# Hybrid Mamba / product-key FFN / linear-attention kernel: the preparation of the FFN stages moved into the stages beside them

## The reference, cut to what matters

```
x = x + mamba(_layernorm(x))          # 512 channels, 16 states, a scan over 1024 steps
x = x + ffn(_layernorm(x))
x = x + linear_attention(_layernorm(x))
x = x + ffn(_layernorm(x))            # the same weights as the first
```

```
queries = (hidden_states @ W_q).reshape(2, n, 64)     # n = 4096 tokens; W_q is 256 x 128
routing = einsum('tnd,tdk->tnk', queries, keys)
scores2, idx2 = top_k(routing, 8)                     # and the best 8 of the 64 pair sums
ew  = silu(einsum('nh,nkh->nk', x, down_embed[indices])) * softmax(scores)
out = einsum('nk,nkh->nh', ew, up_embed[indices])
    + silu(x @ gate_w) * (x @ up_w) @ down_w
```

## Time and profile before

| what | us |
|---|---|
| median of 3 runs | 2038.39 (2036.72 to 2038.93) |
| the profiled execution, its own time | 2038.59 |
| span of its instructions | 2036.9 |
| Mamba ends (last sum into `res`) | 954.54 |
| first matmul of the first FFN loop | 1005.38 |
| last instruction of attention | 1615.51 |
| first matmul of the second FFN loop | 1644.05 |
| PE / DVE / ACT / POOL busy | 1812.9 / 1478.3 / 1054.1 / 1035.7 |

### The profile page before, as it was taken

How to read it: one execution, slowest core, us unless ns; L and a number is a source line. 1 busy time by engine, 2 the same in 40 slices (tenths; PEclk the granted TensorE clock), 3 DMA queues, 4 the chain that set the end, 5 groups by cost and what they waited for, 6 DMA issues and landing times. The chain is left out here.

```text
span 2036.9 us, 27560 instructions
## 1 busy us (share of the span) xinstructions
PE 1812.9 (89%) x9655; PEld 1418.8 (70%) x9655; DVE 1478.3 (73%) x2279; ACT 1054.1 (52%) x1773; POOL 1035.7 (51%) x612
## 2 busy tenths in 40 slices
PE   6888889888989898666799999997999699999999
PEld 2555565656565565455488888886777578888888
DVE  4899999999999999996766666663343555555555
ACT  6775767677776767342444444432333253333333
POOL 2888898989898988874311111111444511111111
PEclk9899999999999999777899999998999899999999
DMA  6222232333323232322000000000000000000000
GB/s 188 76 81 99 85 95 92 90 92 93 93 88 94 91 96 85 93 85 90 0 1 0 0 0 0 0 0 27 1 0 0 0 1 11 10 10 10 10 10 21
DMA packets 55619, 97.78 MB, mean 48 GB/s; under 512 B 10736, under 2 KB 10864, under 8 KB 54896
## 3 DMA queue, kind: packets, MB, share of 16 engines
q1 hardware_dynamic: 55536, 96.74, 15.1%
HBM read 92.00 MB, written 4.72 MB: 47 GB/s over the span
## 5 line engine op out<-in xcount | busy, mean ns | idle before, releaser
L329 POOL TENSOR_TENSOR m_U<-m_U,m_C 128x1024 f32<-128x1024 f32 x256 | 603.5, 2366 | 69.3 <-DVE m_U L751 58.9
L628 ACT ACTIVATE m_dA<-m_delta,m_negA 128x512 f32<-128x512 f32 x512 | 344.4, 685 | 177.0 <-DVE m_U L751 175.1
L456 PEld LDWEIGHTS m_y<-m_ident,m_U 128*128 128x128 f32 x2048 | 258.7, 151 | 114.5 <-issue 72.9
L751 DVE TENSOR_TENSOR_SCAN m_U<-m_dA,m_carry,m_U 128x512 f32<-128x512 f32 x256 | 312.2, 1267 | 7.0 <-ACT m_dA L628 6.6
L456 PE MATMUL m_y<-m_ident,m_U 128*128 128x128 f32 x2048 | 291.9, 290 | 25.5 <-POOL m_U L329 25.4
L751 DVE TENSOR_TENSOR_SCAN m_U<-m_dA,m_U 128x512 f32<-128x512 f32 x256 | 296.9, 1207 | 16.6 <-ACT m_dA L628 13.1
L734 DVE TENSOR_TENSOR m_U<-m_dx,m_psB 128x1024 f32<-128x1024 f32 x208 | 249.3, 1199 | 27.8 <-PE m_psB L440 27.7
L440 PE MATMUL m_psB<-m_stack,m_pick 128*128 128x512 f32 x208 | 110.8, 533 | 66.8 <-DVE m_U L734 66.4
L1100 POOL TENSOR_TENSOR gl_S<-gl_Rt 128x1024 f32<-128x1024 f32 x16 | 31.6, 1997 | 271.5 <-ACT gl_Rt L1208 271.5
L1100 POOL TENSOR_TENSOR fl_S<-fl_Rt 128x1024 f32<-128x1024 f32 x16 | 31.6, 1997 | 264.9 <-ACT fl_Rt L1208 264.9
L1428 POOL TENSOR_TENSOR a_rinv<-a_ssq,a_mhalf 128x64 f32<-128x64 f32 x8 | 84.3, 10550 | 113.5 <-DVE a_ssq L1643 113.5
(11 more groups left out here) (319 smaller groups left out, 4438.0 us busy)
## 6 DMA issues: line engine op xcount, KB each, us to landing
m_C<-bc_rows SPq DMA_DIRECT2D x256, 256.0 KB, 3.1
m_B<-bc_rows SPq DMA_DIRECT2D x48, 256.0 KB, 3.5
fq_whole<-in_ffn_w SPq DMA_DIRECT2D x4, 1024.0 KB, 8.1
out<-res SPq DMA_DIRECT2D x8, 512.0 KB, 2.8
res<-in_x SPq DMA_DIRECT2D x1, 3072.0 KB, 12.6
res<-in_x SPq DMA_DIRECT2D x2, 512.0 KB, 4.6
a_whole<-in_Wkvqu SPq DMA_DIRECT2D x1, 1024.0 KB, 4.8
m_inw<-in_in_w SPq DMA_DIRECT2D x1, 512.0 KB, 4.6
```

What stands on the lines that cost most here:

```text
L329: pool.tensor_tensor(u, u, C[:, M % C_RING, :].unsqueeze(1).to_broadcast([P, PE_E, CHUNK]), ALU.mult).then_inc(hc_ready, 1)
L456: last = nc.tensor.matmul(y[:, t, j * P:(j + 1) * P], U[:, M % U_RING, j, t * P:(t + 1) * P], ident[:, :], start=False, stop=n == N - 1, i ...
L628: nc.scalar.activation(dA[:, s % A_RING, :], delta[:, q, e, :], ACT.Exp, scale=negA[:, e, n:n + 1]).then_inc(dA_ready, 1)
L751: nc.vector.tensor_tensor_scan(u, dA[:, s % A_RING, :], u, carry[:, e, n:n + 1] if q else 0.0, ALU.mult, ALU.add).then_inc(scan_done, 1)
```

## The change

`ffn_queries` is gone. What it did is spread over three places.

1. **In Mamba's chunk 7.** SP fetches `W_q`, `keys` and the four pieces behind C of unit 231 and ahead of C of unit 232. It first waits until the buffers of chunk 6, over which the pieces are written, are free; the last of these waits is for `back3` of chunk 6, which PE does in unit 229. The mean and variance of chunks 4, 1, 5 and 0 are made on ACT (`sum`, `square`), the inverse on POOL (`asked_factors`), and their queries by `norm`, `turn0`, `turn1` and `query` on ACT and PE, at fixed units. `high0` and `high1` round two of the pieces on ACT. The other two are rounded behind the last unit.
2. **At Mamba's end.** DVE makes all four low parts and the low part of the first chunk's `z`. The first half of the output projection is taken ahead of the last two sums over states (`last_out`).
3. **In the FFN loops.** The queries of chunks 2, 6, 3, 7 (first FFN) are made inside loop chunks 1 to 4, and those of 1, 5, 2, 6, 3, 7 (second FFN) inside loop chunks 0 to 5; in the second FFN those of 0 and 4 are made ahead of the loop. The turn stands behind hidden block 1, the multiplication by `W_q` behind block 3, both through `psX`.

To make room, buffers of Mamba, FFN and attention are laid over each other (`Shared`).

```diff
+        "late": [(at + d, name, k) for k, at in ((8, 7), (9, 12), (10, 19), (11, 24))      # PE_AT
+                 for d, name in ((0, "turn0"), (0, "turn1"), (1, "query"))]
+        "late": [(0, "sum", 8), (1, "square", 8), (2, "sum", 9), (3, "square", 9), (6, "norm", 8),   # ACT_AT
+                 (7, "turn0", 8), (7, "turn1", 8), (8, "query", 8), (9, "sum", 10), ...
+        "late": [(2, "clear", 0), (5, "factors", 8), (7, "factors", 9), (14, "factors", 10), (21, "factors", 11)]}  # POOL_AT
+        ASKED = dict(enumerate((4, 1, 5, 0), CHUNKS))
...
+        FETCH = SECOND_LAST + C_RING                       # unit 232
...
+                if M == FETCH:                             # SP
+                    for name in ("back2", "back3"):
+                        wait_full(sp, name, CHUNKS - 2)
+                    sp.wait_ge(nsum_done, SECOND_LAST)
+                    ...
+                    sp.dma_start(shared.wq, dram["W_q"]).then_inc(w_q, 16)
+                    for t in range(2):
+                        sp.dma_start(shared.keyz[64 * t:64 * (t + 1), :, t, :], dram["keys"]).then_inc(w_ffn, 16)
+                    for i in range(PIECES):
+                        sp.dma_start(shared.even[:, i, :], dram["ffn_w"][:, i, :]).then_inc(w_ffn, 16)
...
+            def asked_factors(k):                          # POOL
+                pool.wait_ge(stats_ready, k + 1)
+                pool.wait_ge(rn_ready, k - 1)
+                own.link(pool.tensor_scalar(sc[:, q, 0, :], squares[:, q, :], 1.0 / D, EPS, ALU.mult, ALU.add))
+                own.link(pool.tensor_tensor(norms.inv[:, at, 0], sc[:, q, 0, :], mhalf[:, 0, :], ALU.pow))
+                pool.tensor_scalar(norms.mv[:, at, 0], off[:, q, :], -1.0, None, ALU.mult)
+                pool.tensor_tensor(sc[:, q, 6, :], norms.inv[:, at, 0], off[:, q, :], ALU.mult).then_inc(factors_ready, 1)
...
+            last_out(0, 0)                                 # PE, end of Mamba
             nsum(ALL_UNITS - 2)
+            last_out(1, 0)
             nsum(ALL_UNITS - 1)
-            for name in TAIL_JOBS:
-                part(name, CHUNKS - 1, True)
+            ...  back2 and back3 into psB and dA ...
+            pe.wait_ge(last_free, len(LAST_BACK))
+            last_out(0, 1)
+            last_out(1, 1)
...
+            low(0)                                         # DVE, end of Mamba
             part("gate1", CHUNKS - 1)
+            ...
+            nc.vector.tensor_tensor(shared.zs[:, 1, :, :], rnT, shared.zs[:, 0, :, :].bitcast(FP32), ALU.subtract)
+            low(1)
+            low(2)
             part("out0", CHUNKS - 1)
+            low(3)
             part("out1", CHUNKS - 1)
...
+    ASKED = {1: 2, 2: 6, 3: 3, 4: 7} if first else {0: 1, 1: 5, 2: 2, 3: 6, 4: 3, 5: 7}      # ffn
...
+                    if i == 1 and n is not None:           # PE, FFN loop
+                        pe.wait_ge(zq_ready, Q0 + n + 1)
+                        pe.wait_ge(Rt_ready, c + 1)
+                        turned(psX, zq).then_inc(turnq_full, 1)
+                    if i == 3 and n is not None:
+                        pe.wait_ge(zT_ready, Q0 + n + 1)
+                        asked(psX[:, 0, :], zT).then_inc(q_full, 1)
...
+                    if i == 2 and k is not None:           # ACT, FFN loop
+                        act.wait_ge(turnq_full, Q0 + n + 1)
+                        nc.scalar.activation(zT, psX[:, :, :], ACT.Copy).then_inc(zT_ready, 1)
...
+                    if i == 4 and k is not None:
+                        act.wait_ge(q_full, Q0 + n + 1)
+                        keep(k, psX[:, 0, :])
...
                 low(c, KM - 1)                             # DVE, FFN loop
+                if prepare is not None:
+                    prepare()
...
+                if n is not None:                          # POOL, ahead of its multiplication into W
+                    pool.wait_ge(q_full, Q0 + n + 1)
```

More of the change, by code:

```diff
@@ L389, in part @@
                         out = take(name, k)
-                    last = mm(out, [(w[:, e, :], xs[:, q, e, :])
-                                    for e in (range(KE) if whole else (2, 3) if more else (0, 1))],
-                              not more, more or whole)
+                    last = mm(out, [(w[:, e, :], xs[q][:, e, :])
+                                    for e in ((2, 3) if more else (0, 1))],
+                              not more, more)
                 elif name[:2] == "dt":
@@ L459, in nsum, with last_out @@
                 last.then_inc(nsum_done, 1)
+            def last_out(i, p):
+                if p == 0:
+                    wait_freed(pe, "back1", CHUNKS - 1)
+                    take(f"out{i}", CHUNKS - 1)
+                out = bank(f"out{i}", CHUNKS - 1)
+                for e in range(PE_E * p, PE_E * (p + 1)):
+                    for h in range(2):
+                        last = nc.tensor.matmul(out[:, h * D:(h + 1) * D], in_time(gated[:, e, :])[:, i, h, :],
+                                                outw[:, e, :], start=e == 0 and h == 0, stop=e == KE - 1,
+                                                skip_group_check=True)
+                if p == PASSES - 1:
+                    done(f"out{i}", CHUNKS - 1, last)
             pe.wait_ge(const_ready, 1)
@@ L1336, with attention @@
 Q_SCALE = 0.25
[L1339 removed]
+def attention(nc, res, dram, norms, shared):
     ctx = ExitStack()
```

588 lines of the change are left out of this document (317 added, 271 removed), and 7 rows, old and new, of tables (ACT_AT, PE_AT).

## The result

The changed kernel takes 1992.67 us (median of 4 runs, 1990.91 to 1995.21), the kernel before 2038.15 beside it: ratio 0.9779, 95% interval 0.9762 to 0.9796. I had forecast 2006.3 with a range of 1998 to 2017. The direction and the places were right; the gain is 45.5 us, not 32, and the range was missed.

The account below looks back on a forecast made before the run. PE was taken to bound the FFN loops, so only the two gaps ahead of them could shrink. Terms -50.2 + 6.6 + 3.5 - 2.3 + 10.4 - 15.8 + 15.5 = -32.3 from 2038.59 gave 2006.3 us, range 1998 to 2017.

Parts of the forecast that it names:

- First gap: Between Mamba's last sum and PE's start of the first loop: 50.84 us becomes 0.67, -50.2 us.
- Fetch: Mamba's chunk 7: B of unit 233 waits behind the weight pieces, so DVE scans it later, +6.6 us.
- the fetch costs nothing: Rival for Mamba's chunk 7: C and B come through beside the pieces, 1999.7 us; chance 0.14.
- Queries in chunk 7: Four queries' work on ACT, PE and POOL in Mamba's chunk 7 delays DVE, +3.5 us.
- the next B comes 1 us late: Mamba's chunk 7: DVE's next B is late where no POOL unit follows, two of four queries, 2 us.
- all of it lies under the fetch's wait: Lower bound for the queries in Mamba's chunk 7: they cost 0.
- The rival of 10 us: ACT and PE hold up Mamba's chunk 7: queries 10 for 3.5, fetch 11 for 6.6, 2017.2 us; chance 0.14.
- Mamba's end: From the last gate to the last sum, half the output projection taken earlier: end at 952.2, not 954.54, -2.3 us.
- Questions, 10 x 2.59: FFN loops: each question costs PE a turn and a query, 2.59 us; four +10.4, six +15.5.
- handover: Rival for the loops: PE waits for a copy queued on ACT, 2 us per question, 2026 us; chance 0.10.
- The slower rival: PE's clock falls in the loops for blocks 2 to 4, ten times 8 us, 2086 us; chance 0.03.
- Second gap: Between attention and the second loop: PE starts the loop at 1628.2, not 1644.05, -15.8 us.

Follow-up runs that it names:

- e4: Changed kernel with the four weight pieces issued one at a time behind C of units 233, 235, 237 and 239: 1990.38 us, 1989.75 when run again.
- e6: Changed kernel with only chunk 0's query made in Mamba's chunk 7; those of chunks 4, 1 and 5 left out and made nowhere: 1991.88 us.
- e13: Kernel before with the FFN loop tiles from pause to H, and the weights, at the changed kernel's addresses: 2030.19 us.
- e1: Kernel before with an unused tile of 32 bytes per partition ahead of H in both FFN loops: 2038.44 us, ratio 1.0.
- e5: Changed kernel run once more with nothing changed: 1994.54 us.
- e2: Changed kernel with an unused tile of 32 bytes ahead of H: 1999.26 us.
- e3: Changed kernel with an unused tile of 64 bytes ahead of H: 2000.28 us.
- e12: Changed kernel with an unused tile of 128 bytes ahead of H: 1988.37 us.
- e14: Changed kernel with the small tile csum allocated ahead of W, which moves W by 32 bytes: 1997.7 us.
- e16: Kernel before with an unused tile of 224 bytes ahead of H, putting H at the address 178368: 2024.58 us.

## Why the prediction was wrong, step by step

- *First gap, -50.2.* Right, to 0.1 us: Mamba's last sum is what the loop now waits for.
- *Fetch, +6.6.* Right: DVE waited 5.97 us for POOL, and POOL 8.82 for B. The forecast had B there at 861.5; it was 858.6, since all of chunk 7 ran 3 us earlier. The rival "the fetch costs nothing" fell. e4 shows that its price was the block of four ahead of B, and 4.4 us of it can be had back. Without a query ahead of it the wait is 7.38 us (e6), so 6.6 was if anything low.
- *Queries in chunk 7, +3.5.* The mechanism was there; what was wrong is that it was added to the fetch. I had priced "the next B comes 1 us late" for two of the four, and that happens: 1.05 us at 853.80 in the changed kernel, 0.61 and 1.59 in e4. But in the changed kernel DVE waits for POOL 7 us later in any case, and what it loses ahead of that wait it gains in it: without three of the queries the loop starts at the same place (e6), and no later query costs a wait, the 0.29 us at the silu being 0.29 again. Of 6.6 + 3.5 = 10.1 us together, 7.5 were there. My lower bound, "all of it lies under the fetch's wait", was the right value. The rival of 10 us fell too.
- *Mamba's end, -2.3.* Right (-2.4): DVE's chain behind the gate takes 8.9 us for the 9.5 of the forecast, and the gate comes 1.35 us later behind the last scan for my 0.8. But the old chain from gate to last sum takes 12.6 us in e13 and 14.7 in e1, for 13.9 in the profile that I read, and the new one 10.2 in the changed kernel and in e5: that the two agree to 0.1 us is luck.
- *Questions, 10 x 2.59.* Right (2.60), without a handover to wait for, and with a granted clock of 1.00. The slower rival fell: a turn of 1.03 us and a query in each chunk leave the clock where it is. What I had not thought of is the clock at the loop's first matmuls, 0.50 in the changed kernel and 0.67 before. "TensorE: Matmul & The Clock Gate" of the Trainium skill (part 4, on the transpose mode) says that a transpose doesn't count as activity for the clock the way a matmul does; the window of 1158.83 to 1209.73, at 1.00, shows no harm from it.
- *Second gap, -15.8.* Right (-16.2), and with the six questions of +15.6 this half brings nothing beyond the placement, as said.
- *What had no term.* I took the chunk of 48.70 us as given, as long as no instruction in it changes. That is the step that failed, and it carries 7.4 of the 13.6 us between forecast and median: the change lays H, W and the rest at other addresses, and e2, e3, e12, e14 and e16 show that this alone moves a chunk between 47.95 and 48.87 us. Next come 3.9 us ahead of the fetch in the profile, Mamba's own variation, of the size by which runs of one kernel differ (1991.19 to 1994.88), and then the 2.6 us of queries that the fetch's wait covered.

The range was too narrow for the same reason. Its lower end took in a free fetch and 1.7 us more at Mamba's end, but no term that the change doesn't name. With the output products at their old pace the changed kernel would take about 2000.1 us, and e2 and e3, where an unused tile takes half of the lucky pace away, or more than all of it, take 1999.26 and 2000.28: inside the range of 1998 to 2017, though 6 us below the forecast.

## What to carry to other kernels

Work moved beside another engine's bottleneck is cheap, but ask what covers it: here a wait of 6 to 7 us for the weights hid the queries, and with that wait gone two of four showed, for about 2 us, and the fifth cost most of what it saves. Two delays of one engine ahead of the same wait are not to be added. Work moved beside its own engine's bottleneck cost its duration (2.60 us for 2.59). A block of large transfers should be broken up wherever a small one with a deadline stands behind it in the same queue. When a change moves tiles about in memory, time one loop body against the old one before giving the credit to the change; here a pad of some bytes ahead of what PE loads as weights was worth 0.2 to 0.6%.
